# Projecting the values with one plain float32 product instead of three products of split parts, in an order of its own

## The chip, the cores and the metric

The kernel runs on one core of one Trainium2 chip. The metric is the device time of one execution in microseconds (us), lower is better. Each execution is one launch that works through all 64 sequences of the batch.

## The reference, cut to what matters

Two attention layers in a row, for each of 64 sequences of 128 tokens and width 128. The second layer's values are what the change touches.

```python
# layer 0: cross attention, 16 heads of 8, 77 context tokens
q, k, v = x @ Wq + bq, ctx @ Wk + bk, ctx @ Wv + bv
scores = clip((0.5 * mask + 0.5) * (q @ k.T) / sqrt(8), -50, 50)
x = layernorm(x + softmax(scores) @ v @ Wo + bo) * gamma + beta
# layer 1: self attention in segments of 64 with memory tokens, 16 heads of 64, then a gated feed-forward
xn = rms_norm(x, attn_norm_w)
q, k, v = split(xn @ to_qkv_w, 3)          # 128 -> 3 * 1024
q, k = rope(q), rope(k)
kf, vf = concat([k_extra, pm, k]), concat([v_extra, pm, v])
probs = softmax(where(mask, (q @ kf.T) / 8, -1e30))
x = x + (probs @ vf) @ to_out_w
h = rms_norm(x, ff_norm_w) @ ff_w1 + ff_b1
a, g = split(h, 2)
x = x + (silu(g) * a) @ ff_w2 + ff_b2
```

## The kernel before

One sequence is one step of a software pipeline. The function `pipeline` (line 382) writes, for each of the five engines apart, a loop over turns; in one turn an engine works for up to five sequences at once, each at another stage. `seq[3]` in a body is the sequence three ahead of the turn's number, so a higher lead is an earlier stage. There are `LEAD` (6) turns to fill the pipeline, a loop, and as many to drain it. Inside a turn the order of the work on each engine is written out by hand, and engines meet only through semaphores (`wait_ge` on one side, `then_inc` on the other). The order is therefore fixed per engine, and a late input holds everything behind it on that engine.

The eight banks of the accumulator memory (PSUM) are shared by 33 tasks. The table `tasks` (line 300) gives each its bank, its lead and the semaphore that says that its reader is done; `free` (line 345) makes a task wait for the reader of the task that had the bank before it.

The stages of one sequence, by the names in the table and with TensorE's line numbers:

- `qkv` (L1145 to L1147): projections of the first layer. VectorE makes `kz`, `qb`, `v0` from it.
- `xs0` to `xs3` (L975, `cross_scores`): 16 products on quarters of the array. VectorE multiplies by the mask (L806, `masked`), GpSimd clamps (L501), ScalarE takes exponentials (L652, `exp_cross`).
- `u` (L981, `weigh_cross`), `pv` (L1127), `c0T` (L1029), `wo` (L1038): the rest of the first layer, then its normalisation on VectorE, ScalarE and GpSimd down to `xn`.
- `xnT` (L1068): `xn` is transposed; ScalarE copies it out (L583, `xnT`).
- `k1`, `q1`, `k0`, `q0` (L968, `project_turned`): four float32 products each, which VectorE rotates (L796), with a DMA that swaps neighbouring rows and sums on GpSimd (L495, L497).
- `v0`, `v1` (L961 to L963, `project`): the values, 512 columns each. This is what is changed.
- `scores1`, `scores0` (L990, `scores`): 16 small products each, on top of a mask that ScalarE has laid into the bank (`set_mask`). VectorE takes the largest (L810), ScalarE the exponentials (L626, `exp_self`, four per bank), VectorE their sum, GpSimd the division (L505, L506).
- `turned0` to `turned3` (L998, L999): transposes of the probabilities, which ScalarE copies out (L583, `probsT`, `keep_turned`).
- `o0` to `o3` (L1010, L1016, `weigh`): probabilities times values; ScalarE copies the result (`oT`, `keep_heads`).
- `out` (L1042), `hnT` (L1075), `gate` and `lin` (L1023), `down` (L1111): output projection and feed-forward. For `gate`, ScalarE takes six activations (L646, `gated`).

The values are projected from parts: ScalarE rounds `xnT` to `xnT_hi` in the type float32r, GpSimd subtracts to get `xnT_lo` (L572), and the weights were split the same way once at the start. `project` adds high by high, high by low and low by high:

```python
mm(at(name), xnT_hi[:], wv_hi[:, w], stop=False)
mm(at(name), xnT_hi[:], wv_lo[:, w], start=False, stop=False)
return mm(at(name), xnT_lo[:], wv_hi[:, w], start=False)
```

Of the kernel before, what the change touches and what calls it, by code (L numbers as in the profile page):

```python
# [17 lines left out]
S2 = 77  # L18
# [21 lines left out]
MEANS, POOLED, TOKENS_A, TOKENS_B = 7, 7, 6, 3  # L40
LEAD = 6
# [20 lines left out]
def build(nc, seq_pack, ctx_in, cross_pack, cols_pack, rows_pack, to_qkv_w, to_out_w, persist_mem, to_mem_tokens_w, ff_w1, ff_w2,  # L62
          c_rope, c_tables, out):
    with ExitStack() as ctx:
# [3 lines left out]
        def sem(name):  # L68
# [9 lines left out]
        wv_hi, wv_lo = (sb(n, [D, INNER], F32R) for n in ("wv_hi", "wv_lo"))  # L78
# [40 lines left out]
        xnT_hi, xnT_lo = sb("xnT_hi", [D, S], F32R), sb("xnT_lo", [D, S], F32R)  # L119
# [55 lines left out]
        wv_hi_ready = sem("wv_hi_ready")  # L175
        wv_lo_ready = sem("wv_lo_ready")
# [29 lines left out]
        inputs_in = sem("inputs_in")  # L206
        k0_rotated = sem("k0_rotated")
        k1_filled = sem("k1_filled")
        k1_rotated = sem("k1_rotated")
        lin_filled = sem("lin_filled")  # L210
        mask1_set = sem("mask1_set")
        mask2_set = sem("mask2_set")
# [30 lines left out]
        q0_summed = sem("q0_summed")  # L243
# [3 lines left out]
        qb_ready = sem("qb_ready")  # L247
# [22 lines left out]
        v0_kept = sem("v0_kept")  # L270
# [12 lines left out]
        xnT_hi_ready = sem("xnT_hi_ready")  # L283
# [6 lines left out]
        z0_exp = sem("z0_exp")  # L290
        z0_masked = sem("z0_masked")
        z1_clamped = sem("z1_clamped")
        z1_masked = sem("z1_masked")
# [7 lines left out]
            ("c0T", 0, 4, (c0T_ready,)),  # L301
            ("wo", 3, 4, (y_ready,)),
            ("out", 1, 2, (x1_ready,)),
            ("v0", 0, 3, (vals0_ready,)),
            ("xs0", 5, 5, (z0_masked,)),
            ("xs1", 4, 5, (z1_masked,)),
            ("xs2", 1, 5, (z2_masked,)),
            ("xs3", 6, 5, (z3_masked,)),
            ("scores0", 7, 3, (probs0_exp,)),
            ("v1", 2, 3, (vals1_ready,)),  # L310
            ("scores1", 0, 3, (probs1_exp,)),
            ("xnT", 3, 4, (xnT_ready,)),
            ("lin", 6, 1, (sT_ready,)),
            ("hnT", 1, 2, (hnT_ready,)),
            ("k1", 4, 4, (k1_rotated,)),
            ("q1", 2, 4, (q1_rotated,)),
            ("k0", 5, 4, (k0_rotated,)),
            ("turned2", 0, 3, (probsT2_ready,)),
            ("turned3", 3, 3, (probsT3_ready,)),
            ("q0", 7, 4, (q0_rotated,)),  # L320
            ("u", 4, 5, (u_kept,)),
            ("turned1", 1, 3, (probsT1_ready,)),
            ("down", 6, 1, (out_ready,)),
            ("turned0", 3, 3, (probsT0_ready,)),
            ("gate", 2, 2, (gate_ready,)),
            ("pv", 0, 5, (c0_ready,)),
            ("scores3", 7, 4, (probs3_exp,)),
            ("scores2", 5, 4, (probs2_exp,)),
            ("o0", 6, 3, (oT0_ready,)),
            ("o1", 4, 3, (oT1_ready,)),  # L330
            ("o2", 1, 3, (oT2_ready,)),
            ("o3", 3, 3, (oT3_ready,)),
            ("qkv", 2, 6, (v0_kept,)),
# [64 lines left out]
        def _(sp):  # L398
# [27 lines left out]
            def body(n, seq, done):  # L426
                if seq[3] is not None:
                    sp.wait_ge(k0_rotated, done[4])
                    passed(sp, sp_passed)
                    for odd in range(2):  # L430
                        sp.dma_start(rs[odd::2, half(0)], rb[1 - odd::2, half(0)]).then_inc(swapped0_in, 16)
                    if first(seq[3]):
                        store_memory_values()
                    wait(sp, heads_filled, done[3])
                    passed(sp, sp_passed)
# [13 lines left out]
                if seq[4] is not None:  # L449
                    if first(seq[4]):  # L450
                        other_weights()
# [4 lines left out]
                if seq[6] is not None:  # L456
                    if first(seq[5]):
                        context_loads(2, 3)
                        first_weights()
# [5 lines left out]
                    if first(seq[6]):  # L465
                        context_loads(0, 1)
# [742 lines left out]
```

## Time and profile before

| | us |
|---|---|
| median of 3 runs | 1216.44 (1213.78 to 1217.11) |
| the profiled execution | 1214.23 |
| its span, from the first to the last instruction | 1212.4 |

| engine | busy us | share of the span |
|---|---|---|
| PE (TensorE, products) | 1163.1 | 96% |
| PEld (TensorE, loading of weights) | 1019.5 | 84% |
| ACT (ScalarE) | 1009.3 | 83% |
| POOL (GpSimd) | 993.7 | 82% |
| DVE (VectorE) | 987.0 | 81% |

The granted TensorE clock is 0.996 of full speed over the span. Busy time counts from an instruction's start to its recorded end, and neighbours overlap on PE and ACT, so the distance from one start to the next says more about throughput than the mean duration. The chain of waits is followed back from the last instruction; its pieces lie end to end.

### The profile page before, as it was taken

How to read it: one execution, taken by the hardware profiler on the slowest of the kernel's cores; microseconds unless marked ns; L12 is line 12 of the kernel's file. 1: busy time of each engine (PE TensorE's matmuls, PEld its weight loads, DVE VectorE, ACT ScalarE, POOL GpSimd, SP SyncE). 2: the span in 40 equal slices, each digit the busy share in tenths (PEclk: the TensorE clock that was granted, in tenths of full speed). 3: DMA queues.
4: the chain of work that ended last, by engine and by line, in shares of the span. 5: the costliest groups of instructions: out<-in, count | busy, mean ns of one | idle time of the engine just before them, and what ended most of it. 6: DMA issues, size and time to landing. Idle time of an engine off the chain costs nothing.

```text
span 1212.4 us, 54784 instructions
## 1 busy us (share of the span) xinstructions
PE 1163.1 (96%) x20707; PEld 1019.5 (84%) x20707; DVE 987.0 (81%) x2574; ACT 1009.3 (83%) x3341; POOL 993.7 (82%) x1678
## 2 busy tenths in 40 slices
PE   3799999999999999999999999999999999999985
PEld 2588888888888888888888888888888888888874
DVE  5578888888888888888888888888888888888872
ACT  1488888888888888888888888888888888888874
POOL 1578988888888888888888888888888888888874
PEclk9999999999999999999999999999999999999999
DMA  8122222222232223222222222322222222222220
GB/s 222 59 99 90 84 98 87 82 98 100 69 102 100 80 87 102 86 83 98 87 82 98 91 78 100 102 71 96 102 82 87 98 87 82 98 87 82 99 82 28
DMA packets 54344, 110.43 MB, mean 91 GB/s; under 512 B 9557, under 2 KB 28586, under 8 KB 54186
## 3 DMA queue, kind: packets, MB, share of 16 engines
q1 hardware_dynamic: 54314, 110.01, 27.7%
q8 instruction: 21, 0.34, 0.1%
q14 instruction: 9, 0.07, 0.0%
HBM read 21.63 MB, written 4.46 MB: 22 GB/s over the span
## 4 chain that ended last, share of the span: by engine, by line
PE 91%; DVE 3%; ACT 2%; DMA 1%; issue 1%; POOL 1%; SPq 0%; POOLq 0%; ACTq 0%; DVEq 0%
PE psum L968 18%; PE psum L1042 9%; PE psum L990 7%; PE psum L1023 7%; PE psum L975 6%; PE psum L1010 6%; PE psum L981 5%; PE psum L998 5%; PE psum L1111 4%; PE psum L961 3%; PE psum L1016 3%; PE psum L963 2%; PE psum L1127 2%; PE psum L962 2%; PE psum L999 2%; PE psum L1145 2%
## 5 line engine op out<-in xcount | busy, mean ns | idle before, releaser
L626 ACT ACTIVATE probs<-psum,less_max 128x81 f32<-128x81 f32 x1024 | 236.9, 343 | 50.8 <-DVE less_max L810 50.8
L968 PE MATMUL psum<-xnT,wqkv 128*128 128x128 f32 x2048 | 252.3, 277 | 0.9 <-ACT xnT L583 0.5
L968 PEld LDWEIGHTS psum<-xnT,wqkv 128*128 128x128 f32 x2048 | 240.3, 193 | 1.5 <-DVE z L806 0.7
L505 POOL TENSOR_TENSOR probs_near<-probs,rden 128x256 f32<-128x256 f32 x256 | 157.3, 614 | 71.9 <-DVE rden L894 71.9
L796 DVE TENSOR_TENSOR ra<-psum,rope 128x512 f32<-128x512 f32 x256 | 174.7, 682 | 12.9 <-PE psum L968 5.9
L497 POOL TENSOR_TENSOR kall<-ra,rs 128x512 f32<-128x512 f32 x128 | 162.8, 1272 | 21.2 <-DMA rs<-rb 9.7
L796 DVE TENSOR_TENSOR rb<-psum,rope 128x512 f32<-128x512 f32 x256 | 174.0, 680 | 0.0
L806 DVE TENSOR_TENSOR z<-psum,wT 77x512 f32<-77x512 f32 x256 | 163.7, 679 | 8.4 <-PE psum L975 2.5
L495 POOL TENSOR_TENSOR qT<-ra,rs 128x512 f32<-128x512 f32 x128 | 162.9, 1273 | 0.0
L501 POOL TENSOR_SCALAR z<-z 77x512 f32<-77x512 f32 x256 | 151.6, 609 | 7.9 <-DVE z L806 7.9
L652 ACT ACTIVATE z<-z 77x512 f32<-77x512 f32 x256 | 141.4, 648 | 8.7 <-POOL z L501 8.7
L801 DVE SCALAR_TENSOR_TENSOR kz<-psum,cols 128x308 f32<-128x308 f32 x64 | 34.5, 539 | 118.4 <-PE psum L1147 118.4
L583 ACT ACTIVATE probsT<-psum 128x384 f32<-128x384 f32 x256 | 119.2, 496 | 9.9 <-PE psum L999 4.8
L1042 PE MATMUL psum<-wout,oT 128*128 128x128 f32 x1024 | 125.0, 275 | 1.7 <-ACT oT L583 1.7
L810 DVE TENSOR_REDUCE less_max<-psum 128x4 f32<-128x324 f32 x256 | 116.8, 476 | 10.0 <-PE psum L990 10.0
L1042 PEld LDWEIGHTS psum<-wout,oT 128*128 128x128 f32 x1024 | 119.5, 192 | 2.1 <-ACT oT L583 2.1
L583 ACT ACTIVATE psum<-causal 128x324 f32<-128x324 f32 x256 | 114.9, 449 | 0.1
L990 PEld LDWEIGHTS psum<-kall,qT 64*64 64x64 f32 x4096 | 81.0, 133 | 39.4 <-issue 39.4
L990 PE MATMUL psum<-kall,qT 64*64 64x81 f32 x4096 | 101.9, 236 | 4.7 <-POOL qT L495 2.0
L1023 PE MATMUL psum<-hnT,w 128*128 128x128 f32 (+1 forms) x768 | 106.0, 274 | 0.0
L998 PE MATMUL psum<-cross_w,probs_near 128*128 128x128 f32 x512 | 98.0, 280 | 3.0 <-POOL probs_pre L506 2.3
L583 ACT ACTIVATE oT<-psum 128x256 f32<-128x256 f32 x256 | 83.9, 384 | 12.7 <-PE psum L1016 12.7
(135 smaller groups left out, 2887.7 us busy)
## 6 DMA issues: line engine op xcount, KB each, us to landing
rs<-rb SPq DMA_DIRECT2D x256, 256.0 KB, 2.3
vals_far<-vals SPq DMA_DIRECT2D x128, 128.0 KB, 2.3
seq_in<-in SPq DMA_DIRECT2D x64, 230.5 KB, 2.6
out<-out_sb SPq DMA_DIRECT2D x64, 64.0 KB, 1.6
ctx_all<-in SPq DMA_DIRECT2D x5, 320.0 KB, 9.4
wqkv<-in SPq DMA_DIRECT2D x1, 1536.0 KB, 14.0
vals_pre<-memv_dram SPq DMA_DIRECT2D x64, 4.0 KB
ctx_all<-in SPq DMA_DIRECT2D x3, 288.0 KB, 7.1
```

The costliest lines, as they stand in the source:

```text
L495: return nc.gpsimd.tensor_tensor(qT[:, pairs, :].rearrange("p c i -> p (c i)"), ra[:, sl], rs[:, sl], ALU.add)
L497: return nc.gpsimd.tensor_tensor(kall[:, pairs, :, 0:SEG], *parts, ALU.add)
L505: nc.gpsimd.tensor_tensor(probs_near[:, slots, :], probs[:, slots, 0:SEG], scale.broadcast_to([S, 4, SEG]), ALU.mult)
L583: copy = lambda out, in_, **k: nc.scalar.activation(out, in_, ACT.Copy, **k)
L626: last = nc.scalar.activation(probs[:, 4 * t + n, :], at(f"scores{t}")[:, KEYS * n:KEYS * (n + 1)], ACT.Exp, bias=less_max[:, 4 * t + n:4 ...
L796: last = V.tensor_tensor(dst[:, place(name)].rearrange("p (c i) -> p c i", c=4), p, rope[:, "qk".index(name[0]), n, :].unsqueeze(1).broadc ...
L806: return V.tensor_tensor(z0[:, 4 * t:4 * t + 4, :], at(f"xs{t}")[0:S2, :].rearrange("k (h q) -> k h q", h=4), wT[:].unsqueeze(1).broadcast ...
L968: last = mm(at(name)[:, S * n:S * (n + 1)], wqkv[:, lo + 128 * n:lo + 128 * (n + 1)], xnT[:], start=n == 0)
L990: last = mm(at(f"scores{t}")[queries, KEYS * n:KEYS * (n + 1)], qT[dims, 4 * f + n, queries], kall[dims, 4 * f + n, s, :], start=False)
L998: nc.tensor.transpose(p[:, S * j:S * (j + 1)], pair, ident[:])
L1023: last = mm(at(name)[0:FROWS[n], S * n:S * (n + 1)], w1[:, lo:lo + FROWS[n]], hnT[:])
L1042: last = mm(at("out")[:, 0:D], oT[:, i, :], wout[:, i, :], start=i == 0, stop=i == PAIRS - 1)
```

## The change

The three products become one plain float32 product of 512 columns, straight from `xnT` and `wqkv`. The tiles `xnT_hi`, `xnT_lo`, `wv_hi`, `wv_lo` and the instructions that fill them go away on ScalarE and GpSimd, once per sequence for the input and once per run for the weights. And the turn is written in another order on every engine, with other banks and leads in `tasks`; `LEAD` becomes 7, where the only work of lead 7 is the load of the next inputs on SyncE's queue. `c0T` and `wo` go from lead 4 to 5, the scores and the value projections from 3 to 4, `xs` from 5 to 6, `out` from 2 to 3, `gate` from 2 to 1. The other operations are the same in number and shape. Line numbers are some 15 to 20 lower in the changed file (L583 is L567 there, L626 is L607, L652 is L633, L961 to L963 are L946).

```diff
-MEANS, POOLED, TOKENS_A, TOKENS_B = 7, 7, 6, 3
-LEAD = 6
+MEANS, POOLED, TOKENS_A, TOKENS_B = 2, 2, 0, 4
+LEAD = 7
...
-        wv_hi, wv_lo = (sb(n, [D, INNER], F32R) for n in ("wv_hi", "wv_lo"))
...
-        xnT_hi, xnT_lo = sb("xnT_hi", [D, S], F32R), sb("xnT_lo", [D, S], F32R)
...
         tasks = (
-            ("c0T", 0, 4, (c0T_ready,)),
-            ("wo", 3, 4, (y_ready,)),
...
+            ("gate", 6, 1, (gate_ready,)),
+            ("xnT", 4, 4, (xnT_ready,)),
+            ("lin", 0, 1, (sT_ready,)),
...
-            def value_weight_rest():
-                pool.wait_ge(wv_hi_ready, 1)
-                nc.gpsimd.tensor_tensor(wv_lo[:], wqkv[:, 2 * INNER:], wv_hi[:].bitcast(F32), ALU.subtract).then_inc(wv_lo_ready, 1)
...
-                    pool.wait_ge(xnT_hi_ready, done[5])
-                    nc.gpsimd.tensor_tensor(xnT_lo[:], xnT[:], xnT_hi[:].bitcast(F32), ALU.subtract)
...
-            def value_weight_parts():
-                copy(wv_hi[:], wqkv[:, 2 * INNER:]).then_inc(wv_hi_ready, 1)
...
-                    copy(xnT_hi[:], xnT[:]).then_inc(xnT_hi_ready, 1)
...
             def project(name):
-                w = slice(BANK * int(name[1]), BANK * (int(name[1]) + 1))
-                mm(at(name), xnT_hi[:], wv_hi[:, w], stop=False)
-                mm(at(name), xnT_hi[:], wv_lo[:, w], start=False, stop=False)
-                return mm(at(name), xnT_lo[:], wv_hi[:, w], start=False)
+                lo = 2 * INNER + BANK * int(name[1])
+                return mm(at(name), xnT[:], wqkv[:, lo:lo + BANK])
```

What the order is, at three places. In these rows `out<-in` are the program's tile names, `psum` is the accumulator memory whatever the bank, and the names in brackets are the semaphores that the instruction waits for.

TensorE before, from `wo` and `out` over the two value projections and the cross scores (`qb,kz`) between them:

```order
L1038 MATMUL psum<-cross_w,c0T 128x128 [waits c0T_ready,oT3_ready]
L1042 MATMUL psum<-wout,oT 128x128 [waits oT2_ready]
L1042 MATMUL psum<-wout,oT 128x128 x7
L961 MATMUL psum<-wv_hi,xnT_hi 128x512 [waits c0T_ready]
L962 MATMUL psum<-wv_lo,xnT_hi 128x512
L963 MATMUL psum<-wv_hi,xnT_lo 128x512
L975 MATMUL psum<-qb,kz 77x128 [waits oT0_ready,x1_ready,qb_ready,oT1_ready,probs2_exp]
L975 MATMUL psum<-qb,kz 77x128 x15
L961 MATMUL psum<-wv_hi,xnT_hi 128x512 [waits v0_kept]
L962 MATMUL psum<-wv_lo,xnT_hi 128x512
```

TensorE after, the stretch that holds `out`, both scores and the cross scores, with `v1` last:

```order
L973 MATMUL psum<-kall,qT 64x81 x15
L1105 MATMUL psum<-cross_w,hn 128x128 [waits hn_ready,kz_ready]
L1109 MATMUL psum<-cross_w,c0T 128x128 [waits c0T_ready,c0_ready]
L1114 MATMUL psum<-wout,oT 128x128 [waits oT1_ready,c0T_ready]
L1114 MATMUL psum<-wout,oT 128x128 x7
L973 MATMUL psum<-kall,qT 64x81 [waits k0_summed,mask1_set]
L973 MATMUL psum<-kall,qT 64x81 x15
L958 MATMUL psum<-qb,kz 77x128 [waits out_ready,x1_ready,kz_ready,probs2_exp,hnT_ready]
L958 MATMUL psum<-qb,kz 77x128 x15
L946 MATMUL psum<-wqkv,xnT 128x512 [waits y_ready]
```

Moved: the cross scores now stand straight behind `scores0`, `v0` has gone to a place ahead of `c0T`, and the wait for `probs2_exp` (the exponentials of bank 2 of the self scores) still stands ahead of the cross scores, but `scores1`, on which these exponentials rest, is now written in the same stretch for the same sequence as `scores0`.

ScalarE before, from the exponentials of the cross scores (`z<-z`) to the copies of turned probabilities (`probsT`):

```order
L652 ACTIVATE z<-z 77x512 [waits z3_clamped]
L652 ACTIVATE z<-z 77x512 [waits z2_clamped]
L652 ACTIVATE z<-z 77x512 [waits z1_clamped]
L652 ACTIVATE z<-z 77x512 [waits z0_clamped]
L583 ACTIVATE hnT<-psum,cols 128x128 [waits hnT_filled]
L583 ACTIVATE probsT<-psum 128x384 [waits turned3_filled]
L583 ACTIVATE u<-psum 128x512 [waits uA_filled]
L583 ACTIVATE probsT<-psum 128x384
L583 ACTIVATE probsT<-psum 128x384 [waits turned1_filled]
L583 ACTIVATE probsT<-psum 128x384 [waits turned0_filled]
```

ScalarE after, from the last gate activation to the copy of `u`:

```order
L627 ACTIVATE half_gate<-psum,half_bg 85x128
L633 ACTIVATE z<-z 77x512 [waits z0_clamped]
L567 ACTIVATE wT<-seq_in 77x128 [waits z1_masked,inputs_in]
L567 ACTIVATE probsT<-psum 128x384 [waits turned3_filled]
L633 ACTIVATE z<-z 77x512 [waits z2_clamped]
L567 ACTIVATE probsT<-psum 128x384 [waits turned0_filled]
L633 ACTIVATE z<-z 77x512 [waits z1_clamped]
L567 ACTIVATE probsT<-psum 128x384
L567 ACTIVATE probsT<-psum 128x384 [waits turned1_filled]
L567 ACTIVATE psum<-causal 128x324 [waits k0_rotated]
L567 ACTIVATE u<-psum 128x512 [waits uA_filled]
```

Moved: the exponentials of the cross scores, which stood in a row, are spread between the copies of turned probabilities; the six gate activations stand ahead of all of them, where before they came behind; `u` now comes behind the last of these copies.

TensorE before, from the last turned probabilities to the first products of `weigh` (`probsT,vals`):

```order
L998 MATMUL psum<-cross_w,probs_near 128x128 [waits probs0_ready,probsT3_ready]
L998 MATMUL psum<-cross_w,probs_near 128x128
L999 MATMUL psum<-cross_w,probs_pre 128x128
L1023 MATMUL psum<-hnT,w 128x128 [waits hnT_ready,q1_rotated]
L1023 MATMUL psum<-hnT,w 128x128
L1023 MATMUL psum<-hnT,w 85x128
L1127 MATMUL psum<-cross_w,u 128x128 [waits u_kept,probsT2_ready]
L1127 MATMUL psum<-cross_w,u 128x128 x3
L1010 MATMUL psum<-probsT,vals 64x64 [waits memv_in,vals_far0_in,probsT0_ready,vals_far1_in,probsT1_ready,out_ready,u_kept]
```

TensorE after, from `turned1` to the first products of `weigh`:

```order
L981 MATMUL psum<-cross_w,probs_near 128x128 [waits probs1_ready,q1_rotated]
L981 MATMUL psum<-cross_w,probs_near 128x128
L982 MATMUL psum<-cross_w,probs_pre 128x128
L964 MATMUL psum<-z,v 32x128 [waits z2_exp,gate_ready]
L964 MATMUL psum<-z,v 32x128 x7
L964 MATMUL psum<-z,v 32x128 [waits z1_exp]
L964 MATMUL psum<-z,v 32x128 x7
L993 MATMUL psum<-probsT,vals 64x64 [waits vals_far0_in,memv_in,probsT3_ready,vals_far1_in,probsT2_ready,probsT0_ready,probsT1_ready]
L993 MATMUL psum<-probsT,vals_far 64x64
```

Moved: `gate` and `pv` no longer stand ahead of `weigh`; `u` does. `weigh` waits for the copies of all four turned banks, as before.

## Rows read from the trace of the kernel before

**Rows 1.** The page, part 1: busy time of each engine, share of the span, instructions.

```profile
PE 1163.1 (96%) x20707; PEld 1019.5 (84%) x20707; DVE 987.0 (81%) x2574; ACT 1009.3 (83%) x3341; POOL 993.7 (82%) x1678
```

**Rows 2.** Chain of waits, one steady turn: start us, us, what.

```profile
591.66 1.79 PE psum L1042 x16
593.45 0.23 PE psum L961
...
594.22 1.11 PE psum L975 x32
595.33 0.43 PE psum L961
...
596.23 0.72 PE psum L990 x32
596.95 0.26 PE psum L1068
597.21 0.67 PE psum L1023 x6
...
597.98 2.69 PE psum L968 x24
600.67 0.22 PE psum L998 x2
...
602.22 1.01 PE psum L981 x32
...
603.71 0.67 PE psum L1111 x6
...
605.38 0.44 PE psum L1127 x4
605.81 1.09 PE psum L1010 x64
...
607.52 0.42 PE psum L1145 x2
...
608.46 0.72 PE psum L990 x32
...
609.60 1.79 PE psum L1042 x16
```

**Rows 3.** Timeline, PE, start-up: start us, us, engine line op out<-in xcount [idle before <-releaser].

```profile
46.91 1.07 PE L953 MATMUL psum<-wqkv,memT 128*64 128x512 f32 x2 [1.60 <-ACT memv L583]
```

**Rows 4.** Chain of waits, start-up: the first exponentials.

```profile
53.64 0.51 DVE less_max L810
...
54.17 1.86 ACT probs L626 x8
56.04 0.04 issue
```

**Rows 5.** Timeline, ACT, one steady turn.

```profile
615.58 0.31 ACT L583 ACTIVATE xnT_hi<-xnT 128x128 fp32r<-128x128 f32 x1
615.79 1.84 ACT L626 ACTIVATE probs<-psum,less_max 128x81 f32<-128x81 f32 x8
617.48 2.21 ACT L652 ACTIVATE z<-z 77x512 f32<-77x512 f32 x4
619.56 0.38 ACT L583 ACTIVATE hnT<-psum,cols 128x128 f32<-128x128 f32 x1
...
623.07 0.44 ACT L583 ACTIVATE psum<-causal 128x324 f32<-128x324 f32 x1
623.43 0.36 ACT L646 ACTIVATE tanh_gate<-psum,half_bg 128x128 f32<-128x128 f32 x1
...
624.93 0.46 ACT L583 ACTIVATE psum<-causal 128x324 f32<-128x324 f32 x1
```

**Rows 6.** Timeline, ACT, start-up: the last copies of turned probabilities.

```profile
65.66 1.25 ACT L583 ACTIVATE probsT<-psum 128x384 f32<-128x384 f32 x3
```

**Rows 7.** Chain of waits, start-up, behind those copies.

```profile
66.86 0.47 issue
```

More of the change, by code:

```diff
@@ new lines, in build @@
+            ("o2", 1, 3, (oT2_ready,)),
+            ("o3", 4, 3, (oT3_ready,)),
+            ("down", 0, 1, (out_ready,)),
+            ("scores3", 2, 4, (probs3_exp,)),
+            ("pv", 3, 5, (c0_ready,)),
+            ("qkv", 1, 6, (kz_ready,)),
+            ("v0", 4, 4, (vals0_ready,)),
+            ("c0T", 7, 5, (c0T_ready,)),
+            ("scores0", 4, 4, (probs0_exp,)),
+            ("hnT", 1, 2, (hnT_ready,)),
+            ("wo", 3, 5, (y_ready,)),
+            ("out", 7, 3, (x1_ready,)),
@@ L334, in build @@
+            ("scores1", 2, 4, (probs1_exp,)),
+            ("xs0", 1, 6, (z0_masked,)),
+            ("xs1", 5, 6, (z1_masked,)),
+            ("xs2", 7, 6, (z2_masked,)),
+            ("xs3", 0, 6, (z3_masked,)),
+            ("v1", 3, 4, (vals1_ready,)),
         )
@@ L427, in body @@
                 if seq[3] is not None:
-                    sp.wait_ge(k0_rotated, done[4])
+                    sp.wait_ge(vals0_ready, done[4])
                     passed(sp, sp_passed)
[L430 to L435, printed above, removed]
-                    sp.dma_start(vals_pre[0::BAND, :, :].rearrange("n (f h) d -> n f (h d)", f=2),
-                                 memv_dram[bass.ds(seq[3], 1), :].rearrange("b (f n e) -> (b n) f e", f=2, n=4)).then_inc(memv_in, 16)
+                    sp.dma_start(vals_far[0:SEG, :, :].rearrange("k c e -> k (c e)"), vals[SEG:2 * SEG, 0:BANK]).then_inc(vals_far0_in, 16)
                 if seq[0] is not None:
@@ new lines, in body @@
+                if seq[6] is not None:
+                    if first(seq[5]):
+                        context_totals()
+                    dve.wait_ge(qkv_filled, done[7])
+                    V.tensor_scalar(qb[:], at("qkv")[:, 0:S], cols[:, BQ:BQ + 1], None, ALU.add)
+                    V.tensor_copy(v0[:, :, 0:HD0], at("qkv")[0:S2, 256:384].rearrange("k (h d) -> k h d", h=H))
+                    keys_of_heads().then_inc(kz_ready, 1)
+                    if first(seq[6]):
+                        sum_tokens(0)
+                        sum_tokens(1)
@@ L1140, in body @@
                     weigh().then_inc(heads_filled, 1)
+                if seq[1] is not None:
+                    free(pe, "down", n)
+                    for i in range(FCH):
+                        last = mm(at("down")[:, 0:D], sT[0:FROWS[i], i, :], w2[0:FROWS[i], i, :], start=i == 0, stop=i == FCH - 1)
+                    last.then_inc(down_filled, 1)
+                if seq[5] is not None:
+                    free(pe, "pv", n)
+                    pe.wait_ge(u_kept, done[6])
+                    for g in range(GROUP):
+                        last = nc.tensor.transpose(at("pv")[:, S * g:S * (g + 1)], u[:, S * g:S * (g + 1)], ident[:])
+                    last.then_inc(pv_filled, 1)
                 if seq[6] is not None:
```

607 lines of the change are left out of this document (287 added, 320 removed).

## The prediction, written before the run

> **What bounds the kernel now.** I read the page first: PE is busy 96% of the span, the other three engines with work 81 to 83% [rows 1]. Then the chain of waits over one turn in the middle [rows 2]: it never leaves PE. From the first piece of `out` in one turn (591.66) to that in the next (609.60) a turn takes 17.94 us, and the pieces on PE lie end to end but for under 0.1 us in front of the cross scores. So before, a turn costs what PE needs, and every other engine is early. The timeline of ACT [rows 5] is what I read last, since the new order has to be walked through on it.
>
> **The products themselves.** Before, `v0` takes 594.22 - 593.45 = 0.77 us with the small gap behind it, and `v1` 596.23 - 595.33 = 0.90 [rows 2], together 1.67. After, each is one product of 512 columns. The nearest form in the trace is a float32 product of 512 columns with 64 columns of weights, which shows as 2 records that take 1.07 us from the start of the first to the recorded end of the second [rows 3]. For 128 columns, the pair is 1.79 / 8 = 0.22 us in a row (`out`) [rows 2]; four times the columns is 0.86 to 0.90. I take 0.86, 0.43 per record, because in a stream the tail of the last record overlaps the next one; the upper bound is the 1.07. The Trainium skill, page "FP8 and Floating Point Precision", section "TensorE Precision Notes", says that true float32 takes four passes through the array, so against three products of one pass each the change would lose a third here. By that rule each product would be 4/3 of three pieces of 0.23, 0.92 us, and the turn 0.12 longer than in my sum; the trace agrees in kind, with 0.86 to 0.90 by the rows of `out`.
>
> **Switches between kinds of product.** The chain shows that the first full product behind a group on quarters or halves of the array costs more: `v1`'s first piece is 0.43 where `v0`'s is 0.23, `qkv`'s first 0.42, `xnT` 0.26 [rows 2], so +0.15 to +0.20 each. Before there are five such places in a turn (`wo`, `v1`, `xnT`, `turned1`, `qkv`), after three (`down`, `hnT`, `v1`), because `u` and `weigh`, and `scores0` and the cross scores, now stand back to back. PE's own work in a turn is then 17.94 - 1.67 + (0.86 + 0.86 + 0.20) - (0.20 + 0.15 + 0.15 + 0.20) + (0.20 + 0.15) = 17.84 us. PE alone would gain 0.10 a turn: what the float32 products cost, the order gives back. What decides is whether the others keep PE fed, so I follow the new order around one turn.
>
> **The loop that I find.** Start at `weigh` (time 0).
> 1. PE up to the end of `scores1`: `weigh` 607.52 - 605.81 = 1.71; `down` 0.67 + 0.20; `pv` 0.44; `qkv` and the transpose of `c` 608.46 - 607.52 - 0.20 = 0.74; `v0` 0.86; `scores1` 0.72 [rows 2]. Sum 5.34; +0.07, since a piece of the chain begins only when the one ahead ends. 5.41.
> 2. VectorE takes the largest, 0.51 with 0.02 on each side, then ScalarE 8 exponentials, 1.86 [rows 4]. After, ScalarE lays a mask into bank 2 between the two groups of four, and that mask waits for the first group's end: 623.43 - 623.07 = 0.36 [rows 5], +0.03 for the wait, +0.13 for the overlap of neighbours that is lost (the 8 exponentials show it: 615.79 + 1.84 - 617.48 = 0.15). PE takes the result up after 0.04 [rows 4], and I add 0.08 for one more waiting instruction, an estimate between none and the 0.2 that such a place could take. 0.55 + 1.86 + 0.52 + 0.12 = 3.05. Cross scores start at 8.46. PE by itself would be there at 5.41 + 0.15 + 0.22 + 1.79 + 0.72 = 8.29 (`hnT`, `wo`, `out`, `scores0`), so PE waits for ScalarE by 0.2.
> 3. PE: cross scores 1.11, `v1` 0.86 + 0.20, `gate` 0.67, `xnT` 0.11 [rows 2]. 2.95, at 11.41, with 0.02 to ScalarE.
> 4. ScalarE from the copy of `xnT` on, each by the distance to the next start [rows 5, 6]: `xnT` 0.38 - 0.13 = 0.25 (as `hnT`), four exponentials (617.48 - 615.79) / 2 = 0.85, four of the cross scores 619.56 - 617.48 = 2.08, six gate activations 624.93 - 623.43 = 1.50, `wT` 0.20 to 0.25, four copies of turned probabilities (1.25 - 0.13) / 3 = 0.37 to 0.39 each, 1.5, and 0.13 for the last one's tail. 6.53. All of it is ahead of the copy of `turned1`, for which `weigh` waits.
> 5. From the end of that copy (65.66 + 1.25 = 66.91) [rows 6] PE needs until 66.86 + 0.47 = 67.33 to begin `weigh` [rows 7]: 0.42, in the one turn of the trace where `weigh` came late.
>
> The turn is 8.46 + 2.95 + 0.02 + 6.53 + 0.42 = 18.38 us. PE over the same stretch, with `k1` held until `xnT` is copied, would be about 18.0 to 18.2, so ScalarE's queue is last by some tenths.
>
> **What was hidden.** Before, ScalarE did its gate activations after the turned copies, beside `weigh`, `out` and the score products, and nobody on PE waited [rows 2, 5]. The cover is gone when they stand ahead of these copies: 1.50 us of ScalarE lie on the path. The removed work gives little back. The rounding of `xnT` is 615.79 - 615.58 = 0.21 us of ScalarE [rows 5]; it stood between `xnT` and the exponentials, and its absence is in my sum already. GpSimd's subtraction goes as well; GpSimd has 18% of the span idle [rows 1], and I book nothing. The splitting of the weights at the start was beside PE's start-up work: nothing either. Where the stall at the cross scores goes (for instance with the mask ahead of both groups), ScalarE's chain is next, by the same sum with 8.29 for 8.46: 18.2. The moved DMAs (`rs` swaps, `vals_far`, `vals_pre`, the next inputs) come onto SyncE's queue one or two stages earlier than their readers need them; I book nothing, between -2 and +10 us for the whole run.
>
> **The sum.** +0.44 us a turn over about 61 turns that hold the full load is +27 us. Filling and draining: the same stages, one turn of lead 7 without PE work; between -5 and +5 us, taken as 0. The profiled execution of 1214.2 becomes 1241. Its time is 2.2 below the median of the runs, so the median could be up to 1243; I say 1240.
>
> **The rivals.**
> - *PE stays the bound* (faster). ScalarE has 17% of the span idle [rows 1], and if my distances are each a little long or the reaction times of steps 2 and 5 overlap with PE's own work, the turn falls to PE's 17.84: -0.10 x 61 = -6, about 1208. For it: before, every chain of this kind stayed hidden. Against: step 4 is made of measured distances and misses PE's need by more than one such error. If the two are just level, the turn is 17.9 to 18.0 and the time is 1211 to 1219: no change or nearly.
> - *The product of 512 columns is dearer* (slower still). By the upper bound of 1.07 each [rows 3], twice, minus the 0.86 booked, the loop grows by up to 0.42, as both lie in it: 18.8, 1266. It decides from about 0.9 on. For it: `v0` and `v1` are both on the loop. Against: the pair of records of 128 columns runs at 0.22 in a row.
> - *Another chain is last.* From the cross scores over VectorE's products by the mask, three or four GpSimd steps, and the exponential ahead of `turned2`, I find only 0.2 to 0.3 us less than by ScalarE alone; the rotation of `k0`, its swap and its sum are hidden by about a microsecond. Each could add 0.2 to 0.4 a turn: 1250 to 1265.
> - *The change doesn't do what it says*: the one product still runs as several passes, so it could save no time on PE; that is in the sum already, as 1.92 against 1.67.
>
> **Chances.** The loop through ScalarE as summed, 1226 to 1256: 0.52. PE as the bound, 1204 to 1212: 0.18. Level, 1212 to 1222: 0.15. The dearer product or another chain, 1250 to 1270: 0.15. A difference of 0.3% is 3.6 us, about what a measurement here can tell from no change: faster 0.18, same 0.12, slower 0.70. The range 1209 to 1257 leaves out about 1 in 10 on each side; the likeliest case alone is 1226 to 1256.
>
> **What the profile of the changed kernel would show.** The chain should leave PE in every turn: through VectorE's largest and ScalarE's exponentials to the cross scores, and through ScalarE's exponentials and copies to L993, about 18.4 us from `out` to `out`. PE's share falls to about 94%. L946 has 256 records with some 0.43 us between the two of a pair. An idle time of PE or of its loads in front of L993 and L958 of about 0.2 to 0.4 us a turn, put down to ACT or to issue, shows steps 2 and 5. I am wrong if the turn is under 18.0 us with the chain still on PE alone, if the pair of L946 takes over 0.95 us, or if DVE, POOL or a DMA ends PE's waits.

## The result, and the profile after

The changed kernel takes 1264.91 us in the median (1260.11 to 1265.73), the kernel before 1216.78 (1213.78 to 1221.19) beside it on the same chip: a ratio of 1.038, interval 1.034 to 1.043. Slower, as forecast, but beyond the end of the range (1257) and 25 us above the forecast of 1240. The profiled execution of the changed kernel took 1260.1 us, its span is 1258.3, against 1212.4 before: 45.9 us more.

The page of the changed kernel, part 1, and the group of the new product (columns as in [rows 1]; for the group: busy time, mean ns of one | idle ahead of it):

```profile
PE 1188.2 (94%) x20579; PEld 1020.8 (81%) x20579; DVE 970.4 (77%) x2574; ACT 1000.4 (80%) x3276; POOL 967.0 (77%) x1613
...
L946 PE MATMUL psum<-wqkv,xnT 128*128 128x512 f32 x256 | 138.4, 623 | 0.8 <-DVE y_eps L894 0.6
```

PE is at 94%, as forecast, and the others have more idle time than before [rows 1]. So the answer is not in the shares but in the chain of waits. One steady turn of the changed kernel (start us, us, what), beside [rows 2]:

```profile
593.27 0.30 issue
593.56 1.16 PE psum L993 x64
594.73 0.62 PE psum L999 x32
595.35 0.86 PE psum L1075 x6
...
597.28 0.86 PE psum L946 x2
...
598.97 0.26 PE psum L1105
599.23 0.32 PE psum L1109 x2
...
602.05 1.09 PE psum L958 x32
603.14 1.06 PE psum L946 x2
...
604.86 0.22 PE psum L1017
605.08 0.73 PE psum L1006 x6
605.81 0.94 PE psum L951 x8
...
610.75 1.01 PE psum L964 x32
611.76 0.29 issue
612.05 0.97 PE psum L993 x50
```

The turn is 612.05 - 593.56 = 18.49 us; I had said 18.38. `v0` is 0.86 and `v1` 1.06 (L946), both as in the sum. The chain does not leave PE for VectorE or ScalarE, as I had said it would: it stays on PE, and the only gap is 0.29 to 0.30 us of "issue" ahead of `weigh` (L993), 16.7 us over 56 turns in the table of waits. The wait for ScalarE ahead of the cross scores (step 2 of the prediction) doesn't show either: they begin (L958) 602.05 - 593.56 = 8.49 behind `weigh`, forecast 8.46, but `scores0` runs until then.

ScalarE in the same turn (timeline, columns as in [rows 5]): from the copy of `xnT` to the end of the last copy of turned probabilities.

```profile
605.12 0.37 ACT L567 ACTIVATE xnT<-psum,cols 128x128 f32<-128x128 f32 x1
...
608.76 0.34 ACT L567 ACTIVATE wT<-seq_in 77x128 f32<-77x128 f32 x1
...
610.74 0.91 ACT L567 ACTIVATE probsT<-psum 128x384 f32<-128x384 f32 x2
```

This is 610.74 + 0.91 - 605.12 = 6.53 us, the forecast number, and `weigh` follows 612.05 - 611.65 = 0.40 later (forecast 0.42). But PE's own last piece ahead of `weigh`, `u` (L964), ends at 611.76, later still than that copy, so that the chain names PE and not ScalarE. PE's queue, which runs ahead of the products, tells more. The waits ahead of `weigh` are instructions of their own there. This is what the view of line 349 (`free`) shows for them in this turn, and in a turn of e4 (an experiment below); the three numbers are shortest, median and longest in ns:

```profile
L349 PEldq EVENT_SEMAPHORE  x2: 51/146/240, 611.3 to 611.4; - x2
...
L349 PEldq EVENT_SEMAPHORE  x2: 51/160/269, 594.0 to 594.1; - x2
```

The second of the two takes 0.24 us instead of 0.05. By the records of the trace it lasts from 611.45 to 611.69, 0.04 behind the end of the last copy (611.644), and so in each of 52 steady turns (0.042 to 0.045). So it is this copy that lets PE's queue go on. Three more instructions of the queue (L1067, L1069, L54) follow, which start 0.10 apart, and then `weigh`, in all 0.41 behind the copy. Had the copy been early, they would have run 0.19 sooner, and the gap would have been some 0.10 instead of 0.29 (an estimate from these records). Two paths are nearly level in front of `weigh`, PE's products and ScalarE's queue, and the row of queue instructions stands behind both.

**Where the 45.9 us are.** By the starts of the first L993 (before L1010) of each turn: the first comes at 75.67 instead of 67.33 (+8.3); the 63 turns to the last take 1159.74 instead of 1127.76 (+32.0); from the last to the end it is 22.91 instead of 17.35 (+5.6).

The start-up, chain of waits of the changed kernel:

```profile
10.42 13.80 DMA seq_in<-in
...
24.25 0.31 ACT wT L567
...
25.13 1.98 PE psum L964 x32
...
42.46 6.00 PE psum L951 x32
```

Before, the same L964 (there L981) began at 18.26 and the first product by `wqkv` (L968) at 35.65. Now `wT` of sequence 1 stands in ScalarE's queue ahead of the exponentials of sequence 0, and it waits for inputs that SyncE loads behind the context and the early weights: sequence 0 waits for data of sequence 1.

The end, chain of waits:

```profile
1235.41 1.16 PE psum L993 x64
...
1241.44 0.30 ACT tanh_gate L627
...
1245.81 1.65 PE psum L1075 x6
1247.46 0.23 PE psum L1105
...
1248.22 1.64 PE psum L1006 x6
...
1254.32 1.66 PE psum L1075 x6
```

The transpose of `hn` of the last sequence (L1105) stands on PE behind the `down` (L1075) of the sequence ahead, and this one behind six gate activations, which also stand ahead of `hn` on ScalarE. In the steady state other work fills that place; in the last turns nothing does. From `weigh` to this transpose it is 12.05 us, before 7.19 (1195.09 to 1202.28).

Not all of it is order. The clock granted to TensorE, third number from the right in these lines, is lower from the last `weigh` to the end (start:end, length, busy time of PE, PEld, DVE, ACT, POOL), first before, then changed:

```profile
1195.09:1212.44 17.35, 8.57 (x143) 7.51 (x143) 2.60 (x9) 5.36 (x20) 4.01 (x6) 0.84 0.05 13
1235.41:1258.32 22.91, 12.69 (x156) 10.89 (x156) 3.76 (x13) 5.91 (x22) 4.63 (x8) 0.71 0.03 10
```

In the changed kernel it falls from 1.00 to 0.50 at 1245.1, while PE stands idle (3.8 us, up to 1245.8), and stays there to the end. So `down` takes 1.65, where the same piece takes 0.94 in the end of e3 at the full clock, and the six products by `hnT` take 1.64, before 0.79 (L1023). Before, only the very last `down` (1.66 in both kernels) met this level. The two pieces make some 1.6 of the 5.6 us, by estimate.

### The profile page after: what moved, and what is told of

The parts are those of the page before. It is cut to its first block, busy times and chain, and to the rows that moved or that the text cites. A ratio compares the mean times of both kernels' runs of the same rounds, so it can differ in the third digit from the quotient of the medians.

```text
span 1258.3 us, 54415 instructions
## 1 busy us (share of the span) xinstructions
PE 1188.2 (94%) x20579; PEld 1020.8 (81%) x20579; DVE 970.4 (77%) x2574; ACT 1000.4 (80%) x3276; POOL 967.0 (77%) x1613
## 4 chain that ended last, share of the span: by engine, by line
PE 88%; DVE 4%; DMA 2%; issue 2%; ACT 2%; POOL 1%; SPq 1%; POOLq 0%; DVEq 0%; ACTq 0%
PE psum L951 17%; PE psum L946 9%; PE psum L1114 8%; PE psum L973 7%; PE psum L1006 7%; PE psum L993 6%; PE psum L958 5%; PE psum L964 5%; PE psum L1075 4%; PE psum L981 4%; PE psum L999 3%; PE psum L1081 2%; PE psum L982 2%; PE psum L1109 1%; DMA rs<-rb 1%
## 5 line engine op out<-in xcount | busy, mean ns | idle before, releaser
L951 PE MATMUL psum<-xnT,wqkv 128*128 128x128 f32 x2048 | 265.4, 278 | 1.8 <-ACT xnT L567 1.5
L607 ACT ACTIVATE probs<-psum,less_max 128x81 f32<-128x81 f32 x1024 | 250.2, 329 | 1.4 <-DVE less_max L790 1.4
L951 PEld LDWEIGHTS psum<-xnT,wqkv 128*128 128x128 f32 x2048 | 245.5, 193 | 3.6 <-ACT vals L567 2.2
L633 ACT ACTIVATE z<-z 77x512 f32<-77x512 f32 x256 | 168.2, 658 | 10.3 <-POOL z L490 10.2
L567 ACT ACTIVATE vals<-psum 128x512 f32<-128x512 f32 x128 | 77.2, 604 | 98.1 <-PE psum L946 98.1
L836 DVE RECIPROCAL rden<-psum 128x16 f32<-128x16 f32 x64 | 16.5, 258 | 173.8 <-PE psum L1081 173.8
L946 PE MATMUL psum<-wqkv,xnT 128*128 128x512 f32 x256 | 138.4, 623 | 0.8 <-DVE y_eps L894 0.6
L567 ACT ACTIVATE psum<-causal 128x324 f32<-128x324 f32 x256 | 114.0, 446 | 19.5 <-DVE rb L776 17.4
L567 ACT ACTIVATE probsT<-psum 128x384 f32<-128x384 f32 x256 | 124.0, 524 | 2.8 <-PE psum L982 2.8
L1006 PEld LDWEIGHTS psum<-hnT,w 128*128 128x128 f32 (+1 forms) x768 | 96.7, 181 | 30.6 <-issue 30.6
L1006 PE MATMUL psum<-hnT,w 128*128 128x128 f32 (+1 forms) x768 | 110.6, 281 | 0.6 <-ACT hnT L567 0.6
```

The source lines that it names most:

```text
L567: copy = lambda out, in_, **k: nc.scalar.activation(out, in_, ACT.Copy, **k)
L607: last = nc.scalar.activation(probs[:, 4 * t + n, :], at(f"scores{t}")[:, KEYS * n:KEYS * (n + 1)], ACT.Exp, bias=less_max[:, 4 * t + n:4 ...
L633: return nc.scalar.activation(zt, zt, ACT.Exp, scale=float(HD0) ** -0.5)
L946: return mm(at(name), xnT[:], wqkv[:, lo:lo + BANK])
L951: last = mm(at(name)[:, S * n:S * (n + 1)], wqkv[:, lo + 128 * n:lo + 128 * (n + 1)], xnT[:], start=n == 0)
L1006: last = mm(at(name)[0:FROWS[n], S * n:S * (n + 1)], w1[:, lo:lo + FROWS[n]], hnT[:])
```

## The experiments

Turns below are the median distance between the first L993 of neighbouring turns, from each trace (before, of L1010; "start": the first one; "end": from the last one to the end of the span). Each ratio is to runs of the kernel before beside that experiment, whose medians were 1214.84 to 1217.72.

| kernel | median us | ratio (95%) | start | turn | end |
|---|---|---|---|---|---|
| before | 1216.78 | 1 | 67.33 | 17.93 | 17.35 |
| changed | 1264.91 | 1.034 to 1.043 | 75.67 | 18.49 | 22.91 |
| e1 plain products, old order | 1225.07 | 1.006 to 1.012 | 66.94 | 18.12 | 16.82 |
| e2 split products, new order | 1261.36 | 1.035 to 1.040 | 78.17 | 18.38 | 24.57 |
| e3 changed, one waiting instruction for five | 1248.39 | 1.024 to 1.029 | 75.99 | 18.24 | 24.56 |
| e4 changed, three gate activations fewer | 1256.47 | 1.032 to 1.036 | 76.81 | 18.45 | 20.01 |
| e5 both | 1239.71 | 1.017 to 1.022 | 77.92 | 18.16 | 20.68 |
| e6 changed, wT behind the turned copies | 1258.92 | 1.034 to 1.038 | 74.33 | 18.43 | 22.04 |
| e7 e3 + e6 + split products | 1257.80 | 1.031 to 1.037 | 74.75 | 18.38 | 22.81 |
| e8 before, v1 right behind v0 | 1235.20 | 1.013 to 1.018 | 69.21 | 18.27 | 17.34 |
| e9 e3, wT behind the copy of u | 1238.98 | 1.016 to 1.021 | 70.76 | 18.18 | 22.80 |
| e10 e9 + split products | 1230.02 | 1.009 to 1.013 | 69.43 | 18.02 | 24.58 |
| e11 e8, banks of k1 and q1 exchanged | 1238.32 | 1.015 to 1.021 | 68.75 | 18.27 | 17.47 |

**e1: the products alone.**

```
-                mm(at(name), xnT_hi[:], wv_hi[:, w], stop=False)
-                mm(at(name), xnT_hi[:], wv_lo[:, w], start=False, stop=False)
-                return mm(at(name), xnT_lo[:], wv_hi[:, w], start=False)
+                return mm(at(name), xnT[:], wqkv[:, lo:lo + BANK])
```

> The kernel before with one thing changed: `v0` and `v1` are one float32 product of 512 columns each, and the parts of input and weights are gone; the order on every engine stays that of before. Theory (the price of the products is small, the order is what costs): in the changed kernel v0 takes 0.86 and v1 1.06 us, against 1.67 for both before, so PE, which never waits in the old order, needs 0.25 more a turn. The turn goes from 17.94 to 18.19, the time to 1216.8 + 0.25 x 62 = 1232, between 1228 and 1236, and the start-up and the end stay as they were. Rival (the products are the whole loss): 1260 to 1266. Rival (they sit beside other work): 1214 to 1219.

Chain of waits, e1:

```profile
598.58 0.86 PE psum L939 x2
599.44 1.04 PE psum L951 x32
600.49 1.05 PE psum L939 x2
```

The two products cost 0.86 + 1.05 - 1.67 = 0.24, and the cross scores behind them 0.07 less than the 1.11 of [rows 2]. The turn grows by 0.19 and the median by 9 us, somewhat below the window of 1228 to 1236. A fifth of the loss is the product; the rest is the order. The Trainium skill, page "FP8 and Floating Point Precision", section "TensorE Precision Notes", counts four passes for true float32, which for `v0` meant 4/3 of three pieces, 0.92 by estimate; the trace has 0.86, so the distance of the records in `out` was the better guide.

**e2: the order alone.** The three products back in the changed kernel, the parts made behind the copy of `turned1` (ScalarE) and the sum of `q1` (GpSimd).

```
                     keep_turned(1).then_inc(probsT1_ready, 1)
+                    act.wait_ge(xnT_ready, done[5])
+                    copy(xnT_hi[:], xnT[:]).then_inc(xnT_hi_ready, 1)
...
                     summed("q1").then_inc(q1_summed, 1)
+                    pool.wait_ge(xnT_hi_ready, done[5])
+                    nc.gpsimd.tensor_tensor(xnT_lo[:], xnT[:], xnT_hi[:].bitcast(F32), ALU.subtract).then_inc(xnT_lo_ready, 1)
...
                     free(pe, "v0", n)
+                    pe.wait_ge(xnT_lo_ready, done[5])
```

> The changed kernel with one thing put back: the values come from three products of split parts again. The rounding of xnT stands behind the copy of turned1 on ScalarE, the subtraction behind the sum of q1 on GpSimd, and one more wait stands ahead of v0. Theory (order and products add up): the turn is 18.49 - 0.25 = 18.24, as both products lie on the loop, and the longer start-up and end stay; 1264.9 - 0.25 x 61 = 1250, between 1246 and 1254. Rival (the products are the whole loss): 1215 to 1220. Rival (ScalarE's queue hides the products in part): 1255 to 1264.

1261: a miss of the 1250. PE's pieces of `v0` and `v1` are 0.31 shorter, but the turn only 0.11: the gap ahead of L993 is 0.34 and PE now waits 0.14 more at the transpose of `xn`. And the start is 2.5 us later, with the parts of the weights to be made; but the inputs of sequence 1 also landed 1.4 later (`wT` at 25.63 for 24.25), so how much the parts cost isn't shown. That products and order are not additive was to be cleared up (e7, e10).

**e3 and e4: which of the two level paths.** e3 takes waiting instructions away from the place ahead of `weigh`, e4 work of ScalarE.

The edit of e3 (the three waits for DMAs and a count, `passed`, now stand ahead of `free(pe, "turned1", n)`) and that of e4:

```
-                    free(pe, "o0", n)
-                    free(pe, "o1", n)
-                    free(pe, "o2", n)
-                    free(pe, "o3", n)
-                    pe.wait_ge(vals_far0_in, done[4] * 16)
-                    pe.wait_ge(memv_in, done[4] * 16)
-                    pe.wait_ge(vals_far1_in, done[4] * 16)
+                    pe.wait_ge(probsT1_ready, done[4])
                     passed(pe, pe_passed)
                     weigh().then_inc(heads_filled, 1)
```

```
-                    for dst, function in ((tanh_gate, ACT.Tanh), (half_gate, ACT.Identity)):
+                    for dst, function in ((tanh_gate, ACT.Tanh),):
```

> The changed kernel with one waiting instruction instead of five between the products of `u` and the first of L993: the three waits for DMAs stand ahead of the turns of probs1, and of the four waits for turned copies only that for the last one is left, which ScalarE finishes behind the other three. Theory A (PE's own queue is level with ScalarE's in front of L993: u ends at 611.76 and the waiting instructions take some 0.1 us each): PE's path becomes about 0.3 to 0.4 shorter, but ScalarE's (its copy ends at 611.65) only by what PE needs to get going after it, 0.40 to about 0.1 to 0.2. The turn falls by 0.2 to 0.3, to 18.2 to 18.3; time 1264.9 - 0.25 x 61 = 1250, between 1245 and 1254. Theory B (ScalarE's queue alone with a reaction time that has nothing to do with the number of waits): within 3 us of the changed kernel.

> The changed kernel without three of the six gate activations on ScalarE (the Identity ones, so that the half of the gate's input is left out and the feed-forward adds nothing); about 0.75 us less on ScalarE ahead of its copies of turned probabilities, nothing changed on PE. Theory B (ScalarE's queue is what holds L993): the turn falls until PE's own path is last, by 0.3 to 0.6 us, time 1230 to 1247. Theory A (PE's path through k1, the turns, u and five waiting instructions is level with it): the turn falls by under 0.1, time 1259 to 1265.

Chain of waits around `weigh`, e3:

```profile
605.07 1.01 PE psum L964 x32
606.08 0.04 issue
606.13 1.16 PE psum L993 x64
```

and e4:

```profile
594.50 0.26 issue
594.76 1.16 PE psum L993 x64
```

With one instruction in PE's queue instead of five the gap goes from 0.29 to 0.04, the turn from 18.49 to 18.24, the median by 16.5 us. That much is shown: the row of queue instructions costs 0.25 a turn. `weigh` now begins 0.14 behind ScalarE's last copy (605.98), for 0.41.

With 0.75 us less on ScalarE the gap stays at 0.26 and the turn at 18.45. I took this for theory A on both sides: PE's own work and five instructions set the turn, and ScalarE doesn't. The trace of e4 says otherwise. Timeline of ACT and POOL, same turn as above:

```profile
592.94 0.63 ACT L633 ACTIVATE z<-z 77x512 f32<-77x512 f32 x1
...
593.48 0.84 ACT L567 ACTIVATE probsT<-psum 128x384 f32<-128x384 f32 x2
...
592.30 0.61 POOL L490 TENSOR_SCALAR z<-z 77x512 f32<-77x512 f32 x1
```

The last exponential of the cross scores (`z1`) now stands idle for 0.15 and begins 0.03 behind the end of GpSimd's clamp (592.91); in the changed kernel it followed the work ahead of it without a pause, 0.05 behind that clamp. So the last copy ends hardly earlier (594.32), PE's queue waits for it as before (the 0.27 of the view above), and `weigh` begins 0.44 behind it. A third path, over the cross scores, VectorE's masks and GpSimd's clamps to this exponential, was within 0.1 us of the other two, and e4 only changed which work sets the time of the copy. e4 therefore doesn't show that ScalarE's queue was free of blame. It shows that shortening it alone is worth 0.04. (e4 gained 8 us in the median where 0 to 6 were expected; 2.9 us of it are in the end: 1.5 from the activations in its chain, the rest mostly from PE's pieces there, which ran at a higher granted clock, 0.80 for 0.71 in the mean.)

In the order before, the same queue instructions stood behind `pv` (L1127), and the chain [rows 2] shows no gap: there the last copy ended 0.50 ahead of `weigh`, and the row ran beside `pv`. It costs only where the copy is late.

**e5: both.**

> Both edits together on the changed kernel: three of the six gate activations left out (the Identity ones, so the feed-forward adds nothing), and one waiting instruction instead of five ahead of L993. Theory A (two paths were level in front of L993; with the waiting instructions gone PE itself is the bound, at the 18.24 us a turn that its pieces sum to): the turn is 18.2, within 0.05 of the kernel with few waits alone, and the time 1243 to 1247, the last 3 us from three activations less in the last turns. Theory B (ScalarE still sets a part of the turn): below 18.1 and below 1239.

Chain of waits, e5:

```profile
604.54 1.01 PE psum L964 x32
605.55 1.13 PE psum L993 x64
```

No gap is left, so here PE's products alone are the bound. The turn is 18.16, 0.08 below e3, the median 1239.7, between the two expectations. Of the 0.33 between this and the changed kernel 0.25 go with the queue instructions alone, and 0.08 need less work on ScalarE too. The end is 3.9 us shorter than in e3, again in part by the clock (0.79 for 0.64 in the mean).

**e6 and e9: the start-up.**

The edit of e6; in e9, which has e3's edit too, the same lines stand behind `set_mask(3)`.

```
-                    wait(act, z1_masked, done[6])
-                    copy(wT[:], maskT[:], scale=0.5, bias=0.5).then_inc(wT_ready, 1)
...
                     keep_turned(1).then_inc(probsT1_ready, 1)
+                    wait(act, z1_masked, done[6])
+                    copy(wT[:], maskT[:], scale=0.5, bias=0.5).then_inc(wT_ready, 1)
```

> The changed kernel with the activation that makes wT on ScalarE moved behind the copy of turned1. In the first turns sequence 0 then no longer waits for the inputs of sequence 1 (landed at 24.25, against 18.2 for the first L964 that it holds back), so the first L951 comes at 35.6 to 38 instead of 42.46: 4.5 to 7 us less for the start-up. In the steady turns ScalarE has 0.25 less ahead of its last copy, but PE's own path in front of L993 is level, so 0.05 a turn, 3 us. Time 1264.9 - 3 - 6 = 1256, between 1252 and 1259. Rival (the context loads, whose sums stand next in the chain at 29.52, bind the start-up anyway): 1260 to 1265, with the first L951 above 40.

Chain of waits, e6:

```profile
10.38 15.04 DMA seq_in<-in
...
25.44 0.31 ACT wT L567
25.75 0.49 ACT u L567
```

The theory was right, the edit too timid: now the copy of `u` of sequence 0 stood behind `wT`, and the start gained 1.3 us. The load itself also took 1.2 us longer than in the changed kernel (15.04 for 13.80), as it does by chance between runs: in e3, e4 and e5, which leave the start-up as it was, the first L993 comes at 75.99 to 77.92. The steady turn behaves as expected (-0.06).

> The changed kernel with one waiting instruction ahead of L993, and wT on ScalarE behind the copy of u and the mask of bank 3, where it holds back nothing of the sequence ahead. With wT only behind the copy of turned1, the copy of u of sequence 0 still stood behind it until 25.44 and the start gained 1.3 us. Theory (the start-up's loss is sequence 0 waiting on ScalarE for the inputs of sequence 1): the first L951 comes at 35 to 37 instead of 42.46, the first L993 at about 69; turns stay at 18.24 (PE's own work), so 1248.4 - 6.5 = 1242, between 1239 and 1244. Rival (context loads, first sums or another wait take its place): the first L951 above 39, time 1245 to 1249.

Chain of waits, e9:

```profile
18.76 1.98 PE psum L964 x32
...
36.12 5.23 PE psum L951 x32
```

The first L951 is at 36.12 instead of 42.46 and the first L993 at 70.76 instead of 75.99; the time is 1239.0, in the window. The first L951 is 0.5 from that of the kernel before (35.65), so the loss up to there is this one place in ScalarE's queue. The first L993 is still 3.4 behind. From 40 us to it the granted clock is 0.78 in the mean, for 0.94 before, and `v0` in it takes 1.71 instead of 0.86; how much of the 3.4 is the clock was not tested.

**e7 and e10: products and order together.**

> The changed kernel with three things mended: wT late on ScalarE, one waiting instruction ahead of L993, and the three products of split parts back for the values. If the parts add up: turn 18.24 - 0.24 = 18.0, start-up 6 us shorter: 1248.4 - 15 - 6 = 1227, between 1222 and 1232. If ScalarE's queue becomes last once PE is at 18.0 (its loop was 18.49 with wT in it, so 18.24 now, or 18.0 if its reaction time of 0.42 shrinks with the waits): up to 1240.

Timeline of GpSimd and chain of waits, e7:

```profile
598.21 0.45 POOL L544 TENSOR_TENSOR xnT_lo<-xnT,xnT_hi 128x128 fp32r<-128x128 f32 x1
```

```profile
598.81 0.47 PE psum L962
```

A miss by 30 us, and my own doing: where I had put it, the subtraction ended at 598.66, 0.15 ahead of `v0`, so that PE waited for GpSimd, and `v0`'s first piece was 0.47 instead of 0.23. e10 puts it into the 0.6 us in which GpSimd waits for the swapped rows ahead of the sum of `k1`:

```
                     nc.gpsimd.tensor_copy(kall[:, :, :, SEG:SEG + 1], mk)
+                    pool.wait_ge(xnT_hi_ready, done[5])
+                    nc.gpsimd.tensor_tensor(xnT_lo[:], xnT[:], xnT_hi[:].bitcast(F32), ALU.subtract).then_inc(xnT_lo_ready, 1)
                     pool.wait_ge(swapped1_in, done[5] * 32)
```

> The kernel e9_fill_mended with the three products of split parts back, and with the subtraction for the low part in GpSimd's idle 0.60 us ahead of the sum of k1 (in e7_split_mended it stood behind the sum of q1 and ended at 598.66, and v0 came at 598.81 with a first piece of 0.47). PE's pieces then say 18.18 - 0.14 (v0) - 0.17 (v1) = 17.87; the transpose of xn was level with its input already (5.5 us from wo to xn over VectorE, GpSimd and ScalarE), so 0.05 to 0.15 of that comes back as a wait. Turn 17.92 to 18.05, time 1227 to 1234 with 2 to 3 us more in the start-up for the parts of the weights. Rival (GpSimd's queue, 0.45 longer, is late for the sum of k0 or for the turned probabilities): 18.2 and over, 1240 to 1250.

Turn 18.02, time 1230.0, in the middle of the window: with the two mends the three products are worth 9 us again, as in e1. It is the best kernel in the new order, and still 1.1% slower than before.

**e8 and e11: the price of a switch by itself, in the order before.**

```
                     project("v0").then_inc(v0_filled, 1)
+                    free(pe, "v1", n)
+                    project("v1").then_inc(v1_filled, 1)
...
                     cross_scores().then_inc(xs_filled, 1)
                 if seq[3] is not None:
-                    free(pe, "v1", n)
-                    project("v1").then_inc(v1_filled, 1)
```

> The kernel before (split parts and all) with v1 moved from behind the cross scores to right behind v0, on PE only. It measures the price of a switch by itself: v1's first piece should take 0.23 to 0.25 instead of 0.43, nothing else on PE gets a new switch. The cross scores come 0.75 us later; from the trace of before their last exponential ends at 601.75 and is wanted at about 602.7, so this just fits. Turn 17.94 - 0.15 to 0.20, time 1205 to 1209. Rival (the cross scores' chain over VectorE and GpSimd now comes late for u): 1212 to 1220. Rival (the switch costs nothing by itself): 1215 to 1218.

Chain of waits, e8:

```profile
605.84 0.23 PE psum L961
...
607.72 1.90 DVE z L806 x3
609.66 2.39 PE psum L968 x19
```

`v1`'s first piece is 0.23 instead of 0.43: the price of the switch is right. Yet the kernel is some 20 us slower, since VectorE's products by the mask come 0.75 later, and `k1` behind them. I had followed that delay to the exponentials only. In e11 `k1` has another bank:

> The kernel e8_v1_ahead with the banks of k1 and q1 exchanged, so that k1 goes into the bank that v1 leaves and no longer waits for the third of VectorE's products by the mask (k1 began at 609.66, with that product done at 609.60 and its input copied at 609.27). If that wait is the whole loss, 0.3 of the 18.27 us come back and the turn is 17.95 to 18.0, time 1215 to 1219: the kernel before, no better, since the rest of the gain from the missing switch went into waits of scores0 and k1 on VectorE's later work. If the switch counts in full: 17.75, 1204 to 1207. If VectorE's chain of masks and rotations binds further on: 1225 to 1235.

Chain of waits, e11, from the masks to the divisions ahead of the turn of `probs1`:

```profile
589.97 1.88 DVE z L806 x3
...
595.71 0.41 DVE den L892
...
596.40 0.60 POOL probs_near L505
```

The same 18.27: not the bank but VectorE's row of masks, largest, rotations and sums, which hardly pauses, then held back the turned probabilities (read from the chain, not tested by an edit). A place on PE that saves 0.2 us is worth nothing if it moves the input of such a row by 0.75. The last of the three expectations was nearest, though still too good.

## Why the prediction was right or wrong

- *The products*: right. 0.86 and 1.06 in the trace; alone they cost 9 us. The 1.07 of [rows 3], the upper bound, holds the tail of the last record, which in a row lies beside the next one.
- *Filling and draining, "between -5 and +5 us, taken as 0"*: the step that failed and put the time outside the range. It measured +8.3 and +5.6. I had counted stages instead of walking through ScalarE's queue in the first and last turns, and I had no term for the clock that PE is granted there. What the runs show instead: an instruction for sequence 1 that waits for its load stands ahead of one for sequence 0 (e6, e9; 5.2 of the 8.3), and in the end the transpose of `hn` comes 4.9 later and two groups of products more run at half the clock (some 1.6 of the 5.6). The place of that transpose and the clock are read from the trace, not tested.
- *The loop through ScalarE, 18.38*: right in its last part, and 0.11 too short. By its own steps: 8.49 to the cross scores (forecast 8.46), 3.07 to the copy of `xnT` (2.97 with the 0.02), 6.53 on ScalarE (6.53), 0.41 to `weigh` (0.42). The records of PE's queue show that the copy does release `weigh`. The 3.07 is longer because the transpose of `xn` takes 0.22 for 0.11: its instruction in the queue runs 0.04 behind the end of the copy of `xn` (604.63). In step 2 ScalarE's last exponential ends at 601.93 and PE's queue waits for it until 601.97, 8.41 behind `weigh`, but `scores0` fills PE until 8.49: the agreement with 8.46 is luck in part.
- *PE's own work, 17.84 a turn*: too small by 0.35. Without its gap the turn holds 18.49 - 0.30 = 18.19 of PE pieces. The switches behaved as booked in kind (`down` 0.86, `qkv` without its 0.42, `hnT` 0.26), but pieces that I took over from [rows 2] came out longer at their new neighbours: `weigh` 1.78 for 1.71, `wo` 0.32 for 0.22, `xnT` 0.22 for 0.11, `lin` 0.73 for 0.67, `k1` 0.94 for 0.89. Together 0.39, and 0.04 less elsewhere. Why the others are longer was not tested. In step 2, PE's 8.29 books 0.15 for `hnT`, the switch alone, and leaves out its 0.11.
- *The reaction of 0.42* [rows 7]: right in size, and I didn't ask what it is made of. It is the row of queue instructions. e3 takes 0.25 of it away with one edit.
- *The rivals*: the loop, PE ("level") and "another chain", from the cross scores over GpSimd to the exponential ahead of `turned2`, all lay within a few tenths. e4 shows the third, e5 and e9 (18.16 and 18.18, no gap) show PE alone. I had put the third 0.2 to 0.3 below ScalarE's; in the changed kernel the clamp ended 0.05 ahead of the exponential. The time per turn, forecast +0.44, measured +0.55, makes 32.0 us for 27.
- *The median*: 4.8 us above the profiled execution, where I had allowed for 2.2 and in the end booked none. The granted clock of the profiled execution is 0.992, that of the other three 0.989 to 0.990. With 1241 for 1260.1, a difference of 19.1 is 13.9 for both ends and 5.0 for the turns; rounding is the rest.
- *Signs in the profile*: PE at 94%, L946 with 256 records and the idle time of 0.2 to 0.4 ahead of L993, put down to issue, came. That ahead of L958 did not, nor did "the chain leaves PE": where two paths end about 0.1 us apart, the chain names one of them only.

How the loss comes apart: from the changed kernel 16.5 us go with the waiting instructions (e3), 9.4 with `wT` (e9), 9.0 with the products (e10). The remaining 13 us to the kernel before (14 in the profiled executions) are 0.09 a turn, in all 5, 2 us at the start and 7 at the end, where the granted clock of e10 is 0.64 in the mean for 0.84 before.

## What to carry to other kernels

Where two paths meet within 0.1 us, sum both with the same care, the waiting instructions of the engine's own queue included, and plan the experiment that shortens one at a time. When it gains nothing, look in its trace for what released the wait now, before you acquit the path: a third one may have stood right behind. Put an instruction that waits for many things behind work that is long enough to hide the waits, or let it wait for the last one only. And walk through each in-order queue once for the first and once for the last turns: an instruction for the next sequence that stands ahead of one for this sequence costs little in the middle (0.06 a turn from e3 to e9) and a whole load at the ends.

## What the runs showed of the hardware

Instructions of PE's queue between two groups of products take time when they can't run beside the first: `weigh` begins 0.41 us behind the end of the copy that it waits for with three more of them behind that wait, and 0.14 with none (e3). Their records start 0.10 apart. In the chain they are seen only as "issue". The Trainium skill, page "Perfetto Trace Analysis", section "Per-engine timelines", says that for an instruction of the sequencer alone the profile reports only its execution and not its wait. The traces agree in part: in e3 the record of the last one begins 0.04 behind the copy and takes 0.05, but in the changed kernel a record of 0.24 holds a wait.

The first full product behind a group of small ones costs 0.20 more (0.43 for 0.23 in e8 and before, 1.05 for 0.86 in e1), a transpose there 0.15 (0.26 for 0.11, L1068 in [rows 2]). A float32 product of 512 columns takes 0.43 a record, twice, at a granted clock of 1.00, and 1.71 for the pair where it is 0.50 (`v0` at 54.46 in e9).
